# Attention on one core: transposes and their copies ahead of values and exponentials, the gathered unit right behind the maxima

## The chip, the cores and the metric

The kernel runs on one core of one Trainium2 chip. The metric is the device time of one execution in microseconds (us). Engines are named as in the profile: PE is TensorE's matmul, DVE is VectorE, ACT is ScalarE, POOL is GpSimd, SP is SyncE.

## What is computed

Eight images of 512 channels by 32x32 pixels go through four layers, each with a group norm in front and a residual sum behind. The change lies in the second one, an attention with 8 heads of 64 channels over the 1024 pixels:

```
qkv = einsum('oc,bchw->bohw', qkv_w, x);  q, k, v = split(qkv, 3)      # to heads: b p n d, p = 8, n = 1024, d = 64
rp = (h_pos + w_pos) as p n d
scores = einsum('bpnd,pmd->bpnm', q, rp) + einsum('bpnd,bpmd->bpnm', q, k)
attn = softmax(scores, axis=-1)
out = einsum('bpnm,bpmd->bpnd', attn, v)
x = x + out                                                              # back to channels by pixels
```

The third layer (a deformable convolution) gathers 9 neighbourhoods for each of 16 groups from a table in HBM. The kernel spreads that gather of one image over the stages of others, so it runs beside the attention too.

## The kernel before, in words

**Images and stages.** `program` (L1871) runs image 0 and image 1 through three layers, then a loop over images 2 to 7. From image 1 on, a gather of an earlier image runs beside all stages. The gather is cut into 128 units of 9 indirect DMAs (`Gather`, L90). POOL issues them (`plan`, L131). It is paced by grants: in the attention ACT gives one behind each of its first 8 copies and one with each of the 64 exponentials (`tick`, L324), 72 in all for 30 units (34 in image 1), and POOL's calls are spread evenly over them (270 calls, 3.75 for a grant). Five buffers hold units. POOL waits before a unit until the unit five earlier has been summed (L127). DVE works a unit off in `weigh` (L152): one multiply by the weights (L162) and one reduction (L168), whose end signals `summed`. SP stores a finished tile when its 16 units are summed (`keep`, L177). `Spread` (L228) calls `weigh` so that the units of a stage are spread over its steps.

**The attention** (`layer1`, L989). First a group norm and the values' projection, with ACT copying (L1166). Then 32 steps j: 4 pairs of heads by 8 tiles of 128 queries, both heads r of the pair in one step. Head and tile together make an index i = 2j + r. On four engines, each with an order written out by hand:

- `scores(j)` (PE, L1050): four products for both heads into PSUM banks 0 to 3. It waits until both exponentials of step j-1 are done, as they read the same banks.
- `maximum(i)` (DVE, L1203): negated row maximum of one head's 1024 scores.
- `exponential(i)` (ACT, L1144): exponential with that maximum as bias and the row sum, into one of four tiles E. It gives a grant to POOL.
- `turn(i)` (PE, L1065): eight transposes of E into banks 4 and 5. `turn_copy(i)` takes bank 4 out on DVE (L1210) and bank 5 on ACT (L1134) into ET. The next `turn` writes the same banks, so it waits for both copies.
- `values(c)` (PE, L1075): for a chunk c of two steps, 16 products of vT with ET into bank 6, behind `inverses(c)` (L1091), which spread the inverse row sums in the same bank. `chunk_at(j)` puts them into odd steps from j = 3, the chunk ended two steps earlier.
- `inverse_copy(c)` (ACT, L1155) and `output(c)` (DVE, L1224; in the following even step) take the result out and add it to X.
- `quarter(hp, r)` (PE, L1035): in even steps a quarter of the projection of the next pair's queries and keys into bank 7, taken out by `q_copy` (ACT, L1129) or `k_copy` (DVE, L1190). The last pair has none to make.

A matmul in 32 bits stands in the trace as two instructions, so `scores` is x8, `values` x32 and a quarter x8. The order of one step before:

```
PE    turn(2j-2)  scores(j)  [odd: inverses, values]  turn(2j-1)  [even: quarter]
ACT   copy(2j-2)  exponential(2j)  exponential(2j+1)  [odd: inverse_copy]  copy(2j-1)  [q_copy]
DVE   copy(2j-2)  maximum(2j)  maximum(2j+1)  [invert]  copy(2j-1)  [output]  [k_copy]  spread
```

`turn(2j-2)` and `turn(2j-1)` are of the exponentials of the step before.

Of the kernel before, what the change touches and what calls it, by code (L numbers as in the profile page):

```python
# [17 lines left out]
P = 128  # L18
# [4 lines left out]
PT = N // P  # L23
# [253 lines left out]
class Builder:  # L277
# [711 lines left out]
    def layer1(self):  # L989
        nc, io, PS, X = self.nc, self.io, self.PS, self.X  # L990
        with ExitStack() as ctx:
# [10 lines left out]
            rrow = self.sb(ctx, "rrow", [P, 2 * P])  # L1002
            ov = self.sb(ctx, "ov", [P, 2 * P])
            w_loaded = self.sem("qkv_w_loaded")
            names = ("v_done v_out p_done q_out k_out s_done0 s_done1 max_ready e_ready t_done t_out0 t_out1 o_done0 "
                     "o_done1 rden_ready r_done r_out o_out l1_order").split()
            (v_done, v_out, p_done, q_out, k_out, s_done0, s_done1, max_ready, e_ready, t_done, t_out0, t_out1, o_done0,
             o_done1, rden_ready, r_done, r_out, o_out, order_s) = [self.sem(n) for n in names]
            s_done, o_done = (s_done0, s_done1), (o_done0, o_done1)

            def load(sp):
                sp.dma_start(wq[:], io["qkv_w"][:]).then_inc(w_loaded, 16)
# [17 lines left out]
            with Stage(nc) as block:  # L1030
# [3 lines left out]
                def _(pe):  # L1034
# [29 lines left out]

                    def turn(i):  # L1065
                        pe.wait_ge(e_ready, i + 1)
                        if i:
                            pe.wait_ge(t_out0, i)
                            pe.wait_ge(t_out1, i)
                        for m in range(PT):  # L1070
                            mm = nc.tensor.transpose(PS[:, 4 + m // 4, (m % 4) * P:(m % 4 + 1) * P],  # L1071
                                                     E[i % 4][:, m * P:(m + 1) * P], self.ident[:])
                        mm.then_inc(t_done, 1)

                    def values(c):  # L1075

# [37 lines left out]
                    for j in range(steps + 2):  # L1114
                        if 1 <= j <= steps:
                            turn(2 * j - 2)
                        if j < steps:
                            scores(j)
                        if chunk_at(j) is not None:
                            inverses(chunk_at(j))  # L1120
                            values(chunk_at(j))
                        if 1 <= j <= steps:
                            turn(2 * j - 1)
                        if quarter_at(j):
                            quarter(*quarter_at(j))

                @block.scalar
                def _(act):
                    def q_copy(hp, r):  # L1129
                        act.wait_ge(p_done, 4 * hp + r + 1)  # L1130
                        nc.scalar.activation(q[hp % 2][:, r * NH:(r + 1) * NH], PS[:, 7, :], ACT.Copy)\  # L1131
                            .then_inc(q_out, 1)

                    def turn_copy(i):  # L1134

                        c, r = i // 4, i % 2
                        act.wait_ge(t_done, i + 1)
                        if c >= 2:
                            act.wait_ge(o_done[r], c - 1)
                        nc.scalar.activation(ET[c % 2][r][:, PT // 2:, (i % 4 // 2) * P:(i % 4 // 2 + 1) * P],  # L1140
                                             PS[:, 5, :].rearrange("p (m f) -> p m f", f=P), ACT.Copy)\
                            .then_inc(t_out1, 1)

                    def exponential(i):  # L1144

                        act.wait_ge(max_ready, i + 1)
                        if i >= 4:
                            act.wait_ge(t_done, i - 3)
                        r = i % 2
                        nc.scalar.activation(E[i % 4][:].rearrange("p (h f) -> p h f", h=2),  # L1150
                                             PS[:, 2 * r:2 * r + 2, :], ACT.Exp, bias=nmax[:, i:i + 1],
                                             accum_out=den[:, i:i + 1]).then_inc(e_ready, 1)
                        self.tick(act)

                    def inverse_copy(c):  # L1155

                        act.wait_ge(r_done, 2 * (c + 1))
                        for r in range(2):
                            act.wait_ge(o_done[r], c + 1)
                        if c:  # L1160
                            act.wait_ge(o_out, c)
                        nc.scalar.activation(rrow[:], PS[:, 6, 2 * P:4 * P], ACT.Copy).then_inc(r_out, 1)

                    for m in range(PT):
                        act.wait_ge(v_done, m + 1)
                        nc.scalar.activation(vT[:, m, :], PS[:, m, :], ACT.Copy).then_inc(v_out, 1)  # L1166
                        self.tick(act)
                    for r in range(2):
                        q_copy(0, r)
                    act.wait_ge(v_out, PT)  # L1170
                    for j in range(steps + 2):
                        if 1 <= j <= steps:
                            turn_copy(2 * j - 2)
                        if j < steps:
                            exponential(2 * j)
                            exponential(2 * j + 1)
                        if chunk_at(j) is not None:
                            inverse_copy(chunk_at(j))
                        if 1 <= j <= steps:
                            turn_copy(2 * j - 1)  # L1180
                        if quarter_at(j) and quarter_at(j)[1] < 2:
                            q_copy(*quarter_at(j))

                @block.vector
                def _(dve):
# [23 lines left out]

                    def turn_copy(i):  # L1210

                        c, r = i // 4, i % 2
                        dve.wait_ge(t_done, i + 1)
                        if c >= 2:
                            dve.wait_ge(o_done[r], c - 1)
                        nc.vector.tensor_copy(ET[c % 2][r][:, 0:PT // 2, (i % 4 // 2) * P:(i % 4 // 2 + 1) * P],  # L1216
                                              PS[:, 4, :].rearrange("p (m f) -> p m f", f=P)).then_inc(t_out0, 1)

                    def invert(c):
# [18 lines left out]
                    for j in range(steps + 3):  # L1238
                        if 1 <= j <= steps:
                            turn_copy(2 * j - 2)  # L1240
                        if j < steps:
                            maximum(2 * j)
                            maximum(2 * j + 1)
                        if j >= 2 and j % 2 == 0 and j // 2 - 1 < chunks:
                            invert(j // 2 - 1)
                        if 1 <= j <= steps:
                            turn_copy(2 * j - 1)
                        if j and chunk_at(j - 1) is not None:
                            output(chunk_at(j - 1))
                        if quarter_at(j) and quarter_at(j)[1] >= 2:  # L1250
                            k_copy(*quarter_at(j))
                        if j < steps:
                            spread()
                    spread.end()
                    dve.wait_ge(o_out, chunks)

# [729 lines left out]
```

## Time and profile before

| what | value |
|---|---|
| time of the runs, median of 3 | 17378.5 us (17342.42 to 17394.83) |
| span of the profiled execution | 17321.9 us (its own time outside the span isn't given) |
| busy, share of the span | PE 52%, DVE 56%, ACT 29%, POOL 53% |
| mean granted TensorE clock | 0.726 of full speed |

The busy lines of the page and the slices of the span:

```profile
PE 8991.0 (52%) x32544; PEld 4339.4 (25%) x32544; DVE 9764.5 (56%) x9864; ACT 4946.3 (29%) x13537; POOL 9147.2 (53%) x9221
...
PE   6754554445634564445634555445634556344447
...
POOL 0025655656546664656555664556555665555551
PEclk7976777667766777767866777667866777677778
```

No engine is busy for more than 56% of the span. Each of the 40 slices is 433 us long, so an attention (254 to 440 us) is about one of them, and what bounds it is read from the waits and the order of instructions inside it, not from these shares.

### The profile page before, as it was taken

The numbers are of one execution on the slowest core, as the hardware profiler recorded it, in microseconds if no ns is written. First come the engines' busy times: TensorE is split into PE (matmuls) and PEld (weight loads), VectorE is DVE, ScalarE is ACT, GpSimd is POOL, SyncE is SP. The second block draws the span as 40 slices with busy tenths as digits, with TensorE's granted clock in tenths as the row PEclk, the third lists the DMA queues.
The fourth block names the chain that finished last, engine by engine and source line by source line (L and its number), as shares of the span: only waits on it lengthen the run. The fifth ranks groups of instructions, "written<-read, shape, count | busy, mean of one in ns | idle before, by whom it ended". The sixth has DMA issues, their size and how long they took to land. (4 is left out here: it accounts for less than half of the span.)

```text
span 17321.9 us, 109853 instructions
## 1 busy us (share of the span) xinstructions
PE 8991.0 (52%) x32544; PEld 4339.4 (25%) x32544; DVE 9764.5 (56%) x9864; ACT 4946.3 (29%) x13537; POOL 9147.2 (53%) x9221
## 2 busy tenths in 40 slices
PE   6754554445634564445634555445634556344447
PEld 3322222222312232222312222122312223111113
DVE  7646745476546854477445855467554765433333
ACT  2314421243214421143203422144212432111111
POOL 0025655656546664656555664556555665555551
PEclk7976777667766777767866777667866777677778
DMA  1021112211132112211132112211122111322111
GB/s 58 8 59 42 44 47 66 93 42 51 38 88 66 45 49 62 89 43 52 36 75 79 43 49 59 93 41 46 45 74 78 44 50 51 89 81 71 61 60 45
DMA packets 905633, 1002.04 MB, mean 58 GB/s; under 512 B 697681, under 2 KB 707921, under 8 KB 893074
## 3 DMA queue, kind: packets, MB, share of 16 engines
q0 software_dynamic: 294912, 604.57, 12.3%
q1 hardware_dynamic: 610066, 389.88, 7.4%
q8 instruction: 271, 4.44, 0.1%
q14 instruction: 384, 3.15, 0.1%
HBM read 814.38 MB, written 179.39 MB: 57 GB/s over the span
## 5 line engine op out<-in xcount | busy, mean ns | idle before, releaser
L131 POOL DMA_INDIRECT gat<-corner_tables,idx x9216 | 9146.7, 992 | 7868.6 <-DVE dcn L168 3093.5
L795 PE MATMUL PS<-hc,ident 128*128 128x512 f32 (+2 forms) x4096 | 2018.1, 653 | 483.0 <-DVE hc L839 309.8
L168 DVE TENSOR_REDUCE dcn<-gat 128x32 f32<-128x1152 f32 x1024 | 2162.7, 2112 | 127.2 <-ACT gat L148 83.5
L148 ACT ACTIVATE gat<-gat,wts 128x32 f32<-128x32 f32 x8752 | 1979.4, 308 | 525.6 <-issue 523.8
L862 DVE TENSOR_TENSOR_SCAN hs<-dA,PS 128x1024 f32<-128x1024 f32 x672 | 1531.5, 2279 | 37.5 <-issue 4.4
L162 DVE TENSOR_TENSOR gat<-gat,wts 128x1152 f32<-128x1152 f32 (+3 forms) x1024 | 1093.8, 1068 | 567.1 <-DMA gat<-corner_tables,idx 397.3
L795 PEld LDWEIGHTS PS<-hc,ident 128*128 128x128 f32 x4096 | 1036.8, 286 | 1125.1 <-issue 640.8
L1071 PE MATMUL PS<-ident,E 128*128 128x128 f32 x4096 | 676.5, 313 | 909.1 <-ACT ET L1140 484.0
L1216 DVE COPY ET<-PS 128x512 f32<-128x512 f32 x512 | 348.7, 681 | 1204.6 <-remote 693.6
L839 DVE TENSOR_TENSOR hc<-hs,PS 128x1024 f32<-128x1024 f32 x672 | 803.0, 1195 | 169.7 <-remote 85.6
L1740 PE MATMUL PS<-late_M,wp 128*32 128x512 f32 x4480 | 640.2, 723 | 458.3 <-DVE wp L1804 202.5
L1071 PEld LDWEIGHTS PS<-ident,E 128*128 128x128 f32 x4096 | 528.1, 160 | 1207.9 <-issue 1021.0
L1150 ACT ACTIVATE E<-PS,nmax 128x1024 f32<-128x1024 f32 x512 | 570.0, 1113 | 847.7 <-DVE nmax L1207 508.6
L774 PE MATMUL PS<-bc1f,pick 96*128 96x512 bf16 x1024 | 402.3, 493 | 761.1 <-DVE hc L839 619.2
L774 PE MATMUL PS<-bc1b,pick 96*128 96x512 bf16 x1024 | 391.8, 481 | 779.6 <-DVE hc L839 653.8
L1207 DVE TENSOR_REDUCE nmax<-PS 128x1 f32<-128x1024 f32 x512 | 602.8, 1217 | 273.8 <-PE PS L1060 218.8
L1085 PE MATMUL PS<-ET,vT 128*64 128x256 f32 x4096 | 591.2, 405 | 160.7 <-issue 156.9
L1060 PE MATMUL PS<-kk,q 64*128 64x512 f32 x2048 | 656.9, 771 | 12.8 <-DVE kk L1201 12.8
L1793 DVE COPY row<-PS 128x512 f32<-128x512 f32 x160 | 110.6, 691 | 859.2 <-remote 528.3
L1045 PE MATMUL PS<-XN,wqkv 128*128 128x512 f32 x1024 | 491.8, 625 | 134.9 <-ACT q L1131 66.0
L812 ACT ACTIVATE dA<-delta1f,A 128x1024 f32<-128x1024 f32 x256 | 293.7, 1147 | 838.4 <-DVE hs L862 702.6
L1770 ACT ACTIVATE row<-PS 128x512 f32<-128x512 f32 x160 | 95.5, 597 | 1493.7 <-PE PS L1740 705.9
(251 smaller groups left out, 11848.4 us busy)
## 6 DMA issues: line engine op xcount, KB each, us to landing
gat<-corner_tables,idx POOLq DMA_INDIRECT x9216
corner_tables<-xp SPq DMA_DIRECT2D x1024, 64.0 KB, 2.2
D<-in_dist_dram SPq DMA_DIRECT2D x8, 4096.0 KB, 12.7
keep_scratch<-X SPq DMA_DIRECT2D x15, 2048.0 KB, 11.6
weighted<-M SPq DMA_DIRECT2D x56, 512.0 KB
late_M<-weighted SPq DMA_DIRECT2D x7, 4096.0 KB
wqkv<-in_qkv_w_dram SPq DMA_DIRECT2D x8, 3072.0 KB, 10.2
X<-keep_scratch SPq DMA_DIRECT2D x12, 2048.0 KB, 14.9
```

What stands on the lines that cost most here:

```text
L131: nc.gpsimd.indirect_dma_start(bd.gat[n % self.NG][:, k * 4 * CG:(k + 1) * 4 * CG], None, bd.rows, bass.IndirectOffsetOnAxis(ap=bd.idx[:, ...
L148: ins = nc.scalar.activation(block, block, ACT.Copy, scale=weights[:, i:i + 1])
L162: nc.vector.tensor_tensor(v, v, wv, ALU.mult).then_inc(self.prod, 1)
L168: nc.vector.tensor_reduce(bd.dcn[m % 2][:, g * CG:(g + 1) * CG], gat[:].rearrange("p (k c) -> p c k", c=CG), AX.X, ALU.add).then_inc(self. ...
L774: mm = nc.tensor.matmul(PS[:, bank + i, j * p.hl:(j + 1) * p.hl], self.pick[:, row:row + 1].to_broadcast([3 * BC, P]), p.bc[:, pos], start ...
L795: mm = nc.tensor.matmul(PS[:, p.ybank(d, h), 0:p.hl], self.ident[:], src[:, j, h * p.hl:(h + 1) * p.hl], start=(c == 0 and j == 0), stop=( ...
L839: nc.vector.tensor_tensor(hc[u % 2][:], hs[u % 2][:], Cb, ALU.mult).then_inc(hc_ready, 1)
L862: nc.vector.tensor_tensor_scan(h_, a_, b_, 0.0, ALU.mult, ALU.add).then_inc(scanned, 1)
L1060: mm = nc.tensor.matmul(PS[:, 2 * r + m, :], q[hp % 2][rows, nt * P:(nt + 1) * P], kk[hp % 2][rows, m * NH:(m + 1) * NH], start=True, stop ...
L1071: mm = nc.tensor.transpose(PS[:, 4 + m // 4, (m % 4) * P:(m % 4 + 1) * P], E[i % 4][:, m * P:(m + 1) * P], self.ident[:])
L1207: nc.vector.tensor_reduce(nmax[:, i:i + 1], PS[:, 2 * r:2 * r + 2, :], AX.XY, ALU.max, negate=True).then_inc(max_ready, 1)
L1740: mm = nc.tensor.matmul(PS[32 * j:32 * j + 32, h, :], wp[:, 4 * s + j, :], M[:, 4 * s + j, h * NH:(h + 1) * NH], start=(s == 0), stop=(s = ...
```

## The change

PE's transposes of both indices of a step now stand ahead of inverses and values, and a set of eight is made of two halves, each with its own signal and with a wait for the one copy of its bank. ACT's and DVE's second copies stand ahead of the exponentials and the maxima. DVE's call of `spread` stands behind `output` and ahead of `k_copy`. Which engine takes out which bank, the sizes, the buffers and the numbers of instructions stay, apart from waits.

```diff
@@ -1002,11 +1002,13 @@
             rrow = self.sb(ctx, "rrow", [P, 2 * P])
             ov = self.sb(ctx, "ov", [P, 2 * P])
             w_loaded = self.sem("qkv_w_loaded")
-            names = ("v_done v_out p_done q_out k_out s_done0 s_done1 max_ready e_ready t_done t_out0 t_out1 o_done0 "
+            names = ("v_done v_out p_done q_out k_out s_done0 s_done1 max_ready e_ready t_done0 t_done1 t_out0 t_out1 o_done0 "
                      "o_done1 rden_ready r_done r_out o_out l1_order").split()
-            (v_done, v_out, p_done, q_out, k_out, s_done0, s_done1, max_ready, e_ready, t_done, t_out0, t_out1, o_done0,
+            (v_done, v_out, p_done, q_out, k_out, s_done0, s_done1, max_ready, e_ready, t_done0, t_done1, t_out0,
+             t_out1, o_done0,
              o_done1, rden_ready, r_done, r_out, o_out, order_s) = [self.sem(n) for n in names]
             s_done, o_done = (s_done0, s_done1), (o_done0, o_done1)
+            t_done, t_out = (t_done0, t_done1), (t_out0, t_out1)
 
             def load(sp):
                 sp.dma_start(wq[:], io["qkv_w"][:]).then_inc(w_loaded, 16)
@@ -1064,13 +1066,13 @@
 
                     def turn(i):
                         pe.wait_ge(e_ready, i + 1)
-                        if i:
-                            pe.wait_ge(t_out0, i)
-                            pe.wait_ge(t_out1, i)
-                        for m in range(PT):
-                            mm = nc.tensor.transpose(PS[:, 4 + m // 4, (m % 4) * P:(m % 4 + 1) * P],
-                                                     E[i % 4][:, m * P:(m + 1) * P], self.ident[:])
-                        mm.then_inc(t_done, 1)
+                        for a in range(2):
+                            if i:
+                                pe.wait_ge(t_out[a], i)
+                            for m in range(PT // 2 * a, PT // 2 * (a + 1)):
+                                mm = nc.tensor.transpose(PS[:, 4 + a, (m % 4) * P:(m % 4 + 1) * P],
+                                                         E[i % 4][:, m * P:(m + 1) * P], self.ident[:])
+                            mm.then_inc(t_done[a], 1)
 
                     def values(c):
 
@@ -1116,11 +1118,11 @@
                             turn(2 * j - 2)
                         if j < steps:
                             scores(j)
+                        if 1 <= j <= steps:
+                            turn(2 * j - 1)
                         if chunk_at(j) is not None:
                             inverses(chunk_at(j))
                             values(chunk_at(j))
-                        if 1 <= j <= steps:
-                            turn(2 * j - 1)
                         if quarter_at(j):
                             quarter(*quarter_at(j))
 
@@ -1133,11 +1135,11 @@
 
                     def turn_copy(i):
 
-                        c, r = i // 4, i % 2
-                        act.wait_ge(t_done, i + 1)
+                        c, r, at = i // 4, i % 2, i % 4 // 2 * P
                         if c >= 2:
                             act.wait_ge(o_done[r], c - 1)
-                        nc.scalar.activation(ET[c % 2][r][:, PT // 2:, (i % 4 // 2) * P:(i % 4 // 2 + 1) * P],
+                        act.wait_ge(t_done1, i + 1)
+                        nc.scalar.activation(ET[c % 2][r][:, PT // 2:, at:at + P],
                                              PS[:, 5, :].rearrange("p (m f) -> p m f", f=P), ACT.Copy)\
                             .then_inc(t_out1, 1)
 
@@ -1145,7 +1147,7 @@
 
                         act.wait_ge(max_ready, i + 1)
                         if i >= 4:
-                            act.wait_ge(t_done, i - 3)
+                            act.wait_ge(t_done1, i - 3)
                         r = i % 2
                         nc.scalar.activation(E[i % 4][:].rearrange("p (h f) -> p h f", h=2),
                                              PS[:, 2 * r:2 * r + 2, :], ACT.Exp, bias=nmax[:, i:i + 1],
@@ -1171,13 +1173,12 @@
                     for j in range(steps + 2):
                         if 1 <= j <= steps:
                             turn_copy(2 * j - 2)
+                            turn_copy(2 * j - 1)
                         if j < steps:
                             exponential(2 * j)
                             exponential(2 * j + 1)
                         if chunk_at(j) is not None:
                             inverse_copy(chunk_at(j))
-                        if 1 <= j <= steps:
-                            turn_copy(2 * j - 1)
                         if quarter_at(j) and quarter_at(j)[1] < 2:
                             q_copy(*quarter_at(j))
 
@@ -1209,11 +1210,11 @@
 
                     def turn_copy(i):
 
-                        c, r = i // 4, i % 2
-                        dve.wait_ge(t_done, i + 1)
+                        c, r, at = i // 4, i % 2, i % 4 // 2 * P
+                        dve.wait_ge(t_done0, i + 1)
                         if c >= 2:
                             dve.wait_ge(o_done[r], c - 1)
-                        nc.vector.tensor_copy(ET[c % 2][r][:, 0:PT // 2, (i % 4 // 2) * P:(i % 4 // 2 + 1) * P],
+                        nc.vector.tensor_copy(ET[c % 2][r][:, 0:PT // 2, at:at + P],
                                               PS[:, 4, :].rearrange("p (m f) -> p m f", f=P)).then_inc(t_out0, 1)
 
                     def invert(c):
@@ -1238,19 +1239,18 @@
                     for j in range(steps + 3):
                         if 1 <= j <= steps:
                             turn_copy(2 * j - 2)
+                            turn_copy(2 * j - 1)
                         if j < steps:
                             maximum(2 * j)
                             maximum(2 * j + 1)
                         if j >= 2 and j % 2 == 0 and j // 2 - 1 < chunks:
                             invert(j // 2 - 1)
-                        if 1 <= j <= steps:
-                            turn_copy(2 * j - 1)
                         if j and chunk_at(j - 1) is not None:
                             output(chunk_at(j - 1))
+                        if j < steps:
+                            spread()
                         if quarter_at(j) and quarter_at(j)[1] >= 2:
                             k_copy(*quarter_at(j))
-                        if j < steps:
-                            spread()
                     spread.end()
                     dve.wait_ge(o_out, chunks)
```

## Rows read from the trace of the kernel before

**Rows 1.** The page's first line.

```profile
span 17321.9 us, 109853 instructions
```

**Rows 2.** Windows, first to last exponential of an attention: images 0, 5, sum of eight.

```profile
core 0: us, PE busy (x) PEld busy (x) DVE busy (x) ACT busy (x) POOL busy (x), PEclk, DMA share, GB/s
710.10:964.30 254.20, 226.18 (x1425) 131.87 (x1425) 132.97 (x178) 117.96 (x210) 0.00 (x0) 0.97 0.00 1
...
10258.10:10667.00 408.90, 275.10 (x1423) 153.47 (x1423) 215.44 (x228) 116.64 (x209) 224.74 (x227) 0.80 0.13 38
...
sum 3121.10, PE 2146.78 PEld 1200.81 DVE 1650.57 ACT 936.13 POOL 1598.90; mean PE 268.35 PEld 150.10 DVE 206.32 ACT 117.02 POOL 199.86
```

**Rows 3.** Waits of DVE and ACT, whole span: us in total, times, longest.

```profile
DVE ET L1216 <- remote: 693.6, 81, 14.2
...
DVE nmax L1207 <- remote: 35.5, 22, 4.2
...
ACT rrow L1162 <- remote: 734.1, 80, 17.6
```

**Rows 4.** Timeline of image 0, an odd and an even step: start, us, engine, line.

```profile
742.13 1.04 PE L1071 MATMUL PS<-ident,E 128*128 128x128 f32 x8
...
743.10 1.99 PE L1060 MATMUL PS<-kk,q 64*128 64x512 f32 x8
...
745.02 0.66 PE L1099 MATMUL PS<-ident,rden 128*64 128x128 f32 x8
745.12 2.35 DVE L1207 TENSOR_REDUCE nmax<-PS 128x1 f32<-128x1024 f32 x2 [0.77 <-PE PS L1060]
745.50 3.62 PE L1085 MATMUL PS<-ET,vT 128*64 128x256 f32 x32
746.38 1.11 ACT L1150 ACTIVATE E<-PS,nmax 128x1024 f32<-128x1024 f32 x1 [2.57 <-DVE nmax L1207]
...
749.06 1.09 PE L1071 MATMUL PS<-ident,E 128*128 128x128 f32 x8
...
750.19 0.69 DVE L1216 COPY ET<-PS 128x512 f32<-128x512 f32 x1 [2.71 <-PE PS L1071]
...
754.82 3.60 PE L1045 MATMUL PS<-XN,wqkv 128*128 128x512 f32 x8
755.25 1.11 ACT L1150 ACTIVATE E<-PS,nmax 128x1024 f32<-128x1024 f32 x1 [2.57 <-DVE nmax L1207]
...
758.26 0.82 PE L1071 MATMUL PS<-ident,E 128*128 128x128 f32 x6
```

**Rows 5.** Timeline of image 5, from an even step's exponential to the next one's.

```profile
10413.62 1.11 ACT L1150 ACTIVATE E<-PS,nmax 128x1024 f32<-128x1024 f32 x1 [3.36 <-DVE nmax L1207]
...
10417.65 1.41 POOL L131 DMA_INDIRECT gat<-corner_tables,idx  x1 [0.30 <-issue]
...
10418.17 1.35 DVE L162 TENSOR_TENSOR gat<-gat,wts 128x1152 f32<-128x1152 f32 x1
10419.36 0.97 POOL L131 DMA_INDIRECT gat<-corner_tables,idx  x1 [0.30 <-issue]
...
10421.59 0.68 DVE L1216 COPY ET<-PS 128x512 f32<-128x512 f32 x1
...
10423.44 1.11 ACT L1150 ACTIVATE E<-PS,nmax 128x1024 f32<-128x1024 f32 x1 [5.14 <-DVE nmax L1207]
10423.55 1.09 PE L1071 MATMUL PS<-ident,E 128*128 128x128 f32 x8
...
10431.88 0.94 POOL L131 DMA_INDIRECT gat<-corner_tables,idx  x1 [0.30 <-issue]
10435.58 0.69 DVE L1216 COPY ET<-PS 128x512 f32<-128x512 f32 x1 [11.04 <-remote]
...
10436.64 1.94 PE L1071 MATMUL PS<-ident,E 128*128 128x128 f32 x8 [11.99 <-ACT ET L1140]
10438.51 3.65 PE L1060 MATMUL PS<-kk,q 64*128 64x512 f32 x8
...
10443.45 1.11 ACT L1150 ACTIVATE E<-PS,nmax 128x1024 f32<-128x1024 f32 x1 [4.24 <-DVE nmax L1207]
```

## Prediction, made before the result

> **What bounds the kernel now.** I read the page's span first [rows 1], then the windows from the first to the last exponential of each image's attention [rows 2]. The reader is to see that image 0, which has no gather beside it, needs 254.2 us for 32 steps, and image 5, taken as the type of the other seven, 408.9 us. All eight make 3121.1 us, so the seven take 2866.9 us, 18% of the span with image 0: that is all the change can touch. PE's busy time differs little (226 and 275 us), so the 155 us between them are mostly waits.
>
> The waits say which [rows 3]. VectorE's copy of transposes (L1216) waited 693.6 us in 81 places for a signal that came long after the instruction that sends it ("remote"), and ScalarE's inverse copy (L1162) 734.1 us in 80. The maxima (L1207) waited in this way only 35.5 us. Both long waits are for PE work behind or in the values. I call such a place a hold, and count 80 of them in 7 images of 16 chunks (a chunk is two steps, an odd one with values and an even one): 80 chunks with a hold, 32 without, and 16 in image 0.
>
> The timelines give the anatomy. In image 0 [rows 4], one chunk runs from the first transposes of an odd step at 742.13 to those two steps later at 758.26: 16.13 us. PE is in it nearly all the time, but the odd step's second transposes stand behind values (749.06), and their two copies (750.19) stand between them and the next step. In image 5 [rows 5] the same transposes are issued at 10423.55, their copy starts at 10435.58. In between POOL issues gather calls, the last at 10431.88; the signals came 3.70 us after that. I read a hold as ending with POOL's run, and a run as ending when the calls granted by the two exponentials of each step are used up. So one held chunk is POOL's run plus the way from the release to the next even step's exponential, 10435.58 to 10443.45: 7.87 us. After the hold PE is also at the lower clock level (1.2 GHz): eight transposes take 1.94 us for 1.04 to 1.09, scores 3.65 for 1.99.
>
> **The change, part by part.** Nothing is added or removed but waits: the same matmuls, copies and gather units in another order. No DMA is moved on a queue; the unit's end signal, which lets POOL reuse a buffer and SP store a finished tile, comes earlier. Durations are of the profiled execution, whose span is 17321.9 us; the page gives no time outside it, and I take the 56.6 us by which the median of the runs (17378.5) lies above as unchanged.
>
> *Without a gather.* From the start S of the scores in an odd step: PE goes on 1.92 later (743.10 to 745.02), now with transposes 0.97 (742.13 to 743.10), inverses 0.48, values 3.56 (745.50 to 749.06), and the next first transposes 0.97, whose copies nothing waits for: the next scores start at S+7.90. In an even step the projection takes 3.44 (754.82 to 758.26): 1.92+0.97+3.44+0.97 = 7.30. The other way is longer than now but not last: half a set of transposes gives its copy 1.13-4x0.12 = 0.64 after the start (749.06 to 750.19 is 1.13 for eight), so VectorE copies at S+2.56, its maxima start at S+3.25 instead of S+2.02 (0.69 for the copy), the exponential 1.26 behind (745.12 to 746.38), and two of 1.11 end at S+6.7 [rows 4]. Sum 15.20 for 16.13: 0.93 x 16 chunks = **15 us** less. Here a wait of 2.7 us (copies behind values) goes, and PE itself is late next.
>
> *A chunk without a hold, with a unit in each step.* Odd to even: now 8.87 (746.38 to 755.25), plus 1.00, since the unit (10418.17 to 10421.59, 3.42) starts behind the copy at 750.88, ends at 754.30 and puts another copy in front of the maxima due at 753.99, 1.26 ahead of 755.25 [rows 4, 5]: 9.87. Changed: maxima end 1.09 behind the exponential's start, unit to 4.51, copy to 5.20, PE free for the second transposes at 7.90-4.51+1.92 = 5.31, then 0.64+0.69+1.26: 7.90. Gain 1.97. Even to odd the unit costs more: between it and the next maxima stand two copies and half a set of transposes (0.69+0.64+0.69), where one copy stood, and one copy left the place ahead of it: 2.02-0.68-0.68 = 0.66 lost on today's 9.82 (10413.62 to 10423.44). Net 1.3 x 32 = **42 us** less. The projection's copy for keys, now behind the unit, was behind or ahead of it on the same engine and still ends before the copies; ScalarE's second copy, now queued ahead of the exponentials, waits for transposes that end before the maxima do, so the exponentials do not see it.
>
> *A held chunk.* The trace shows no step in this order under a hold, so I bound it. At the release the copies of the odd step are done, for its transposes now stand ahead of values. What remains depends on how far PE got. If it issued one more set of transposes behind values, as it does now at 10423.55, then scores 3.65, half a set 0.64, copy 0.69, maxima 1.26 remain: 6.24 for 7.87, gain 1.63. If the scores got through as well: two copies 1.38, half a set at the lower clock 0.97, maxima 1.26: 3.6, gain 4.2. If the transposes did not get through, 1.87 more than the first: 8.11, loss 0.24. I take the first, which is what that row shows: 1.63 x 80 = **130 us** less, ends +340 and -19.
>
> *Given back in held chunks.* A unit that today often stands behind a release, with POOL at rest, will stand inside POOL's run. Beside the multiply (10418.17) one call took 1.41 and the next came 1.71 later, against 0.94+0.30 [rows 5]: 0.47 per unit, at one unit a chunk **37 us** more; ends 0 and the whole multiply, 1.35 x 80 = 108. The Trainium skill (SBUF — State Buffer, "Who interferes with whom") says that a tensor_tensor has no two-port mode and takes only the read interface, while writing descriptors needs the write one, so the gather should not feel it: by that rule this term would be 0 and the forecast 37 us lower; the row disagrees, and I keep the row. And the 0.66 of the even step puts the odd exponentials at 10.5 behind the even ones, after POOL has used the first grant; this matters where the step also has a key copy, half of them: 0.66 x 40 = **26 us** more (ends 0 and 53).
>
> Sum: 15+42+130-37-26 = 124 us less, 17378.5-124 = 17254.5, forecast **17255**. A difference under 0.3% (52 us) is about what a measurement of this kernel can't tell from none.
>
> **The rivals.** *Holds swallow the gain.* They stop PE before the transposes behind values, the way from release to exponential is 8.11, and the two losses stay: 15+42-19-37-26 = -25, so 17404. For it: a hold begins somewhere in the values, and PE issues nothing behind 10423.55 for 12 us. Against: that set itself was issued at full speed. Chance 0.20.
>
> *Slower: the copy ahead of the maxima is caught.* The maxima now stand behind a copy that needs PE's signal from the half set behind the scores. If a hold begins that early, some forty matmuls sooner than today, the odd exponentials wait for the end of the even step's grant: calls for 7.5 x 1.25 = 9.4 us, release 12.2 behind the even exponential, odd exponentials at 14.1 (0.69+1.26); their own grant then holds values until 26.3, and 6.24 on: 32.5 for 29.83. That is 2.7 x 80 = 216 slower, less 57 gained elsewhere, plus 37: 17575. Against: signals of the scores, eight matmuls earlier, are hardly ever late (35.5 us, against 693.6) [rows 3]. Chance 0.11.
>
> *Holds become rarer,* since odd exponentials come later, POOL's run breaks and PE's signals flow in the break: half of them gone is 40 x 8.6 (693.6/81) = 344, with the rest some 470 us: 16910. Nothing in the rows shows that a break of under 1 us is enough. Chance 0.07.
>
> **How the numbers follow.** The forecast has 0.62. It reaches up to 15+42+340 = 397 less (16981); the first rival and the spread of the runs (17342.4 to 17394.8, 26 each way) carry the upper end to 17440. Left out are the slower rival and the rare holds, 0.18. Faster by over 0.3%: 0.58 of the forecast (the small rest falls within) and 0.07, 0.65. Within: 0.04 and 0.14 of the first rival, 0.18. Slower: the rest of that, 0.06, and 0.11, 0.17.
>
> **What would show it.** Image 0's window near 239 us, with the maxima's start 3.2 behind the scores and no wait of L1216 or L1140 for transposes behind values. In the others the remote wait of L1216 in odd steps should now fall on the next step's first copy, the unit (L162) should stand beside POOL's run during a hold, and from the release to the next exponential there should be 6.2 us. I am wrong if the maxima show long remote waits (slower rival), if first transposes start only after the release (first rival), if there are clearly fewer than 80 holds, or if POOL's run does not end where the hold ends.

## The result, and the profile after

The changed kernel took 17246.6 us (median of 5 runs, 17184.8 to 17253.2) against 17378.5 us before: ratio 0.9926, 95% interval [0.9907, 0.9945]. The forecast was 17255 us. That the total agrees doesn't show that its terms do, so they are checked one by one below.

First the page of the changed kernel, its span and its busy line:

```profile
span 17245.0 us, 109853 instructions
...
PE 9108.0 (53%) x32544; PEld 4392.2 (25%) x32544; DVE 9764.0 (57%) x9864; ACT 4950.1 (29%) x13537; POOL 9165.7 (53%) x9221
```

The instructions are the same in number, and so is the work of VectorE and ScalarE. The span is 77 us shorter than in the profile of before [rows 1], the median 132 us: the profiled execution of before was one of its quicker ones. Only 1.6 us of the changed kernel's profiled run (17246.6 us) lie outside its span, so the 56.6 us that the forecast put there were mostly scatter between executions.

The windows from first to last exponential of images 0 and 5, and the sum of all eight, which answer to [rows 2]:

```profile
711.30:955.40 244.10, 230.17 (x1435) 134.72 (x1433) 132.33 (x179) 119.80 (x210) 0.00 (x0) 0.96 0.00 1
...
10205.00:10613.70 408.70, 299.86 (x1435) 162.82 (x1433) 217.04 (x230) 118.19 (x210) 227.07 (x231) 0.80 0.13 38
...
sum 3091.20, PE 2288.71 PEld 1255.61 DVE 1663.05 ACT 948.76 POOL 1638.41; mean PE 286.09 PEld 156.95 DVE 207.88 ACT 118.60 POOL 204.80
```

Image 0 fell by 10.1 us, the sum by 29.9 us. What follows the last exponential up to the last output (from its start, in the timelines) fell by another 39 us over the eight images (238.3 to 199.3 us). In a second pair of profiles, below, it fell by 16 us (230.9 to 214.9).

Then the waits of the changed kernel, to be held against [rows 3]:

```profile
DVE ET L1217 <- remote: 978.5, 125, 19.7
...
DVE nmax L1208 <- PE PS L1062: 17.1, 8, 2.1
...
ACT rrow L1164 <- remote: 845.6, 87, 22.0
```

The maxima hardly wait any more, as their own engine now comes late instead (the second copy stands in front of them). The copies wait longer for late signals than before, and in more places: 125 instead of 81, and the inverse copies in 87 instead of 80. The holds did not get rarer; they got more.

The timeline of image 0, an odd step and the beginning of two even ones' scores, against [rows 4]:

```profile
745.88 1.99 PE L1062 MATMUL PS<-kk,q 64*128 64x512 f32 x8
...
747.80 1.09 PE L1073 MATMUL PS<-ident,E 128*128 128x128 f32 x8
748.49 0.69 DVE L1217 COPY ET<-PS 128x512 f32<-128x512 f32 x1 [1.36 <-PE PS L1073]
...
749.10 2.35 DVE L1208 TENSOR_REDUCE nmax<-PS 128x1 f32<-128x1024 f32 x2
749.31 3.62 PE L1087 MATMUL PS<-ET,vT 128*64 128x256 f32 x32
...
752.86 1.09 PE L1073 MATMUL PS<-ident,E 128*128 128x128 f32 x8
...
753.88 1.99 PE L1062 MATMUL PS<-kk,q 64*128 64x512 f32 x8
...
761.13 1.13 PE L1062 MATMUL PS<-kk,q 64*128 64x512 f32 x4
```

From the odd step's scores the next ones follow after 8.00 us (forecast 7.90), and the next after 7.25 (7.30); the maxima start 3.22 behind the scores (3.25). PE runs through without a gap.

The timeline of a held chunk, here in image 6, against [rows 5]:

```profile
12304.27 1.11 ACT L1152 ACTIVATE E<-PS,nmax 128x1024 f32<-128x1024 f32 x1 [0.35 <-DVE nmax L1208]
...
12310.48 1.06 PE L1073 MATMUL PS<-ident,E 128*128 128x128 f32 x8 [0.75 <-DVE ET L1217]
...
12311.96 3.74 PE L1087 MATMUL PS<-ET,vT 128*64 128x256 f32 x30
...
12314.02 1.35 DVE L162 TENSOR_TENSOR gat<-gat,wts 128x1152 f32<-128x1152 f32 x1
...
12314.91 1.27 POOL L131 DMA_INDIRECT gat<-corner_tables,idx  x1 [0.30 <-issue]
...
12316.49 0.94 POOL L131 DMA_INDIRECT gat<-corner_tables,idx  x1 [0.30 <-issue]
...
12317.14 0.81 PE L1073 MATMUL PS<-ident,E 128*128 128x128 f32 x3
...
12321.57 4.05 PE L1062 MATMUL PS<-kk,q 64*128 64x512 f32 x5
12322.73 0.94 POOL L131 DMA_INDIRECT gat<-corner_tables,idx  x1 [0.30 <-issue]
12326.01 2.08 PE L1062 MATMUL PS<-kk,q 64*128 64x512 f32 x3 [0.39 <-issue]
12326.27 0.69 DVE L1217 COPY ET<-PS 128x512 f32<-128x512 f32 x1 [8.77 <-remote]
...
12329.78 2.35 DVE L1208 TENSOR_REDUCE nmax<-PS 128x1 f32<-128x1024 f32 x2
...
12331.03 1.11 ACT L1152 ACTIVATE E<-PS,nmax 128x1024 f32<-128x1024 f32 x1 [0.35 <-DVE nmax L1208]
```

The second transposes (12310.48) are out of the way before values. The unit runs during the hold, beside POOL's run. Behind values PE does not stand still: it lets the next eight transposes (three of them shown) and five of the eight matmuls of the next scores through, a few at a time. The release at 12326.27 comes 3.54 us after the last call of the run, and the next exponential 4.76 us after the release, where it took 7.87 in the chunk of [rows 5].

### The profile page after: what moved, and what is told of

Read it like the earlier page. It is cut to its first block and busy times, and to the rows that moved or that the text cites. A ratio compares the mean times of both kernels' runs of the same rounds, so it can differ in the third digit from the quotient of the medians.

```text
span 17245.0 us, 109853 instructions
## 1 busy us (share of the span) xinstructions
PE 9108.0 (53%) x32544; PEld 4392.2 (25%) x32544; DVE 9764.0 (57%) x9864; ACT 4950.1 (29%) x13537; POOL 9165.7 (53%) x9221
## 5 line engine op out<-in xcount | busy, mean ns | idle before, releaser
L862 DVE TENSOR_TENSOR_SCAN hs<-dA,PS 128x1024 f32<-128x1024 f32 x672 | 1531.8, 2279 | 36.0 <-DVE PS L830 4.6
L1073 PE MATMUL PS<-ident,E 128*128 128x128 f32 x4096 | 713.6, 315 | 726.3 <-DVE ET L1217 297.3
L1062 PE MATMUL PS<-kk,q 64*128 64x512 f32 x2048 | 708.3, 761 | 48.1 <-issue 33.3
L1142 ACT ACTIVATE ET<-PS 128x512 f32<-128x512 f32 x512 | 305.5, 597 | 1222.0 <-PE PS L1073 576.4
L1047 PE MATMUL PS<-XN,wqkv 128*128 128x512 f32 x1024 | 535.6, 672 | 132.7 <-issue 70.2
```

What stands on the lines that cost most here:

```text
L862: nc.vector.tensor_tensor_scan(h_, a_, b_, 0.0, ALU.mult, ALU.add).then_inc(scanned, 1)
L1062: mm = nc.tensor.matmul(PS[:, 2 * r + m, :], q[hp % 2][rows, nt * P:(nt + 1) * P], kk[hp % 2][rows, m * NH:(m + 1) * NH], start=True, stop ...
L1073: mm = nc.tensor.transpose(PS[:, 4 + a, (m % 4) * P:(m % 4 + 1) * P], E[i % 4][:, m * P:(m + 1) * P], self.ident[:])
```

## Experiments

Two theories stood at the start. Theory 1 is the forecast's: the gain is the shorter way from the end of a hold to the next exponential, and holds end with GpSimd's run of calls. Theory 2, the rival: the gain comes from VectorE's unit, whose earlier end frees a gather buffer sooner; over the whole span GpSimd's wait for the unit's reduction fell from 3093 to 2827 us.

Ratios are to the kernel before, run in the same session; sessions differ (it took 17162 us in the first of these, 17354 and 17362 in the others, and 17378 with the result), so total times are compared as ratios. Where holds are counted, a hold is an odd step whose inverse copy starts over 3 us after the exponential in front of it ended, in the timeline of images 1 to 7. Only chunks with another step behind them are counted, 14 in each image, 98 in all: behind the last two of an image no exponential follows in that attention. (The 84 holds and the 6.3 us of the expectations take in most of these as well.) "The way" is from the inverse copy's start to the next exponential, the median over the holds. The even-to-odd steps are 98 too, the first ones of each image's 15.

### Both kernels a second time

> The kernel before, unchanged, as a second profiled sample. Both theories: no difference in time (17340 to 17395 us), eight attentions from first to last exponential of 3080 to 3150 us in sum, inverse copies held in 60 to 75 places, and about 7.9 us from a release to the next exponential. If its attentions scatter by more than 60 us against the first profile, the sums of single profiles cannot carry an argument of that size.

> The changed kernel, unchanged, as the control for the others. 17185 to 17255 us; eight attentions of 3050 to 3110 us in sum from first to last exponential; 80 to 90 held inverse copies with a median of 6.3 us from the release to the next exponential, in two groups near 3.6 us (the next scores went through during the hold) and 6.5 us (they did not).

The kernel before: ratio 0.9998 [0.998, 1.0016], 61 holds (55 in the first profile), way 7.96 us (7.96). The changed kernel: 0.9926 [0.9901, 0.9951], the same as the first time, 77 holds (74), way 4.69 us (6.22). The sums of the windows, before and then changed:

```profile
sum 3118.60, PE 2136.54 PEld 1195.95 DVE 1650.16 ACT 938.10 POOL 1601.19; mean PE 267.07 PEld 149.49 DVE 206.27 ACT 117.26 POOL 200.15
```

```profile
sum 3013.10, PE 2248.81 PEld 1240.29 DVE 1664.99 ACT 950.70 POOL 1633.18; mean PE 281.10 PEld 155.04 DVE 208.12 ACT 118.84 POOL 204.15
```

This pair differs by 105.5 us, the first by 29.9: the changed kernel's own two profiles are 78 us apart, more than expected. So no sum of one profile is used below to weigh a part under 80 us. The two groups of ways are there: in the first profile of the changed kernel 21 of 74 lie between 3 and 4 us and 25 between 6 and 7; in the second 34 of 77 and 12. They stand at the forecast's two cases, 3.6 and 6.24 us.

Not all holds end some 3 to 4 us behind a run. The medians from the start of the last call to the release are 3.75 and 3.79 us in the kernel before and 3.62 and 3.32 in the changed one, but 13 of 55 and 15 of 61 holds, then 14 of 74 and 20 of 77, end less than 2 us after the start of a call, many of them in the middle of a run. No run here shows what ends these.

### The unit alone

```diff
# the kernel before, VectorE's loop
+                        if j < steps:
+                            spread()
                         if 1 <= j <= steps:
                             turn_copy(2 * j - 1)
...
-                        if j < steps:
-                            spread()
```

> The kernel before with only VectorE's gathered unit moved, right behind the maxima and ahead of the second copy; PE, ScalarE and the transposes as before. Theory 1 (the gain is the shorter way from a hold's release to the next exponential, because the odd step's copies are done before the hold): that way stays at 7.9 us, image 0 stays at 253 us, time within 0.3% of before, 17330 to 17430 us. Theory 2 (the gain is the earlier unit, which frees a gather buffer sooner, as GpSimd's wait for the unit's reduction fell from 3093 to 2827 us): most of the gain shows, 17240 to 17300 us, and that wait falls by 200 us or more.

Ratio 1.0023 [1.0005, 1.0041]: slightly slower. GpSimd's wait is down all the same, and the windows are longer:

```profile
POOL gat L131 <- DVE dcn L168: 2652.5, 373, 50.4
```

```profile
sum 3208.10, PE 2126.07 PEld 1210.05 DVE 1667.93 ACT 941.24 POOL 1683.18; mean PE 265.76 PEld 151.26 DVE 208.49 ACT 117.66 POOL 210.40
```

The wait fell by 244 us against the same kernel in that session (2896.1) and the time did not fall with it. So a shorter wait for the unit does not by itself bring time, and theory 2 has no support here. It is not quite out: the way did not stay at 7.9 us as theory 1 had it, but rose to 9.52, so about 1.6 us in each of 80 holds may hide a gain. That the unit now stands ahead of the copy for which the next transposes wait is the likely reason, and was not tried by itself.

The run shows something else: the unit alone brings more holds, 80 for 55 and 61. GpSimd's wait for a buffer beside image 5's attention is, in the two profiles of the kernel before, in this run and in the changed kernel:

```profile
POOL gat L131 <- DVE dcn L168: 61.4, 9, 16.7
...
POOL gat L131 <- DVE dcn L168: 57.7, 8, 16.8
...
POOL gat L131 <- DVE dcn L168: 15.9, 6, 7.4
...
POOL gat L131 <- DVE dcn L168: 29.0, 5, 14.6
```

Over images 1 to 7 it is 418 and 393 us before, 112 here, and 147 and 151 in the two profiles of the changed kernel: with buffers free sooner, GpSimd's runs have fewer breaks. And here 49 of the 80 holds end less than 2 us after the start of a call, so that most of them do not end behind a run.

### The set of eight in one piece, and the unit behind the key copy

```diff
# the changed kernel, PE (the copies' waits follow)
-                        for a in range(2):
-                            if i:
-                                pe.wait_ge(t_out[a], i)
-                            for m in range(PT // 2 * a, PT // 2 * (a + 1)):
+                        if i:
+                            pe.wait_ge(t_out0, i)
+                            pe.wait_ge(t_out1, i)
+                        for m in range(PT):
...
```

> The changed kernel with the set of eight transposes in one piece again: one signal after all eight, both copies awaited before the next set. Theory 1: VectorE's second copy and with it the maxima come 0.5 us later at full clock and 1.0 us at the lower one, so the way from a release to the next exponential grows from 6.3 to about 7 us, and 84 holds with some unheld steps give 40 to 90 us: 17270 to 17330 us; image 0 stays within 3 us, as PE is last there. Theory 2 (the unit's place makes the gain): no difference to the changed kernel, 17185 to 17255 us.

Ratio 0.9939 [0.9917, 0.996]. The way's short group moved from 3 to 4 us (21 of 74 holds) to 4 to 5 us (21 of 54), as if the half set saved about a microsecond there; image 0 took 245.6 us for 244.1. In time it is 0.13% (22 us) behind the changed kernel, less than expected and within both intervals: what the split is worth stays open. The holds lie elsewhere, too: 54 in odd steps, but 36 even-to-odd steps over 13 us, where the changed kernel had 19 and 12.

```diff
# the changed kernel, VectorE's loop
-                        if j < steps:
-                            spread()
                         if quarter_at(j) and quarter_at(j)[1] >= 2:
                             k_copy(*quarter_at(j))
+                        if j < steps:
+                            spread()
```

> The changed kernel with VectorE's unit behind the copy of keys again, as before, in the steps that have one. Theory 1: the unit is off the path of a hold, and in unheld even steps it ends before or after the key copy with the same sum, so no difference to the changed kernel: ratio 0.990 to 0.995 to before. If the unit's place carries the gain, it is lost in a fourth of the steps: ratio 0.994 to 0.998.

Ratio 0.9951 [0.9932, 0.997], on the border of the two expectations, and the interval overlaps the changed kernel's: not told apart either.

### Finer grants

```diff
# the changed kernel, ScalarE
-                self.background(block, self.share["attention"], ticks=PT + 2 * steps)
+                self.background(block, self.share["attention"], ticks=PT + 4 * steps)
...
                             .then_inc(t_out1, 1)
+                        self.tick(act)
```

> The changed kernel with a grant for GpSimd also behind each of ScalarE's transpose copies: 136 grants instead of 72 for the same 270 calls, so that the two odd exponentials release 4 calls instead of 7.5. Theory 1 (a hold ends when GpSimd's run ends): about 4.4 us less run behind the odd exponentials in some 84 holds, 200 to 370 us less in the attentions and a time of 16880 to 17050 us. If holds last as long as they do for a reason of PE's own, whatever GpSimd does: no difference, 17185 to 17255 us, and releases no longer follow the last call by 3.6 us.

16933.3 us, ratio 0.9753 [0.9732, 0.9773]: 0.9753/0.9926 = 0.983 of the changed kernel, some 300 us, as theory 1 expected.

```profile
sum 2881.90, PE 2230.69 PEld 1242.72 DVE 1662.06 ACT 946.34 POOL 1741.66; mean PE 278.84 PEld 155.34 DVE 207.76 ACT 118.29 POOL 217.71
```

The windows are 131 and 209 us shorter than in the two profiles of the changed kernel. From the first value copy to the first exponential it is 401.1 us for 524.5 and 516.5, about 120 us less: there each grant released 3.75 calls, now 2. So only part of the some 300 us comes from holds. Their number is about the same (73 for 74 and 77), and the median one still ends 3.33 us after a call, but the run behind the odd exponentials is shorter: an odd-to-even step with a hold takes 15.9 us in the mean for 18.7 and 18.1. No instruction of PE, VectorE or the gather was changed, only when GpSimd may issue. So how long a hold lasts depends on the run.

The same on the kernel before:

> The kernel before with the finer grants of the previous experiment alone (136 for the same 270 calls, the new ones behind ScalarE's transpose copies). Theory 1: holds end with GpSimd's run in this order too, so the part from the first value copy to the first exponential falls by 110 to 125 us in sum as it did there, and the loops by some 100 to 200 us: ratio 0.980 to 0.987 to before. The changed order still wins on top, since the way from a release to the next exponential stays near 7.9 us here (4.6 us there): slower than the changed kernel with fine grants (ratio 0.975) by 60 to 150 us. If the finer grants make the order immaterial, 0.973 to 0.977.

Ratio 0.9841 [0.9819, 0.9862], with a way of 7.52 us against 3.98: much as theory 1 expected. The finer grants are worth 1.6% in the old order, and the new order is worth 0.9% on top (0.9753/0.9841 = 0.991; the intervals are apart).

### All grants of a chunk at the even step's copies

```diff
# the finer grants, ScalarE
-                        self.tick(act)
+                        if i % 4 >= 2:
+                            for _ in range(4):
+                                self.tick(act)
...
                                              accum_out=den[:, i:i + 1]).then_inc(e_ready, 1)
-                        self.tick(act)
```

> The changed kernel with as many grants (136), but those of a chunk all at the two copies of its even step, four each, and none with the exponentials, so that one run of 15 calls starts right behind the release. Theory 1: a chunk is then the run (18.75 us and 0.5 for each unit beside it), 0.7 ahead of it and 3.6 behind it, 23 to 24 us, against 26.3 in held chunks of the fine grants: 50 to 130 us less than those, ratio 0.968 to 0.973. If what counts is how many PE instructions fall into one run, the run now meets scores, transposes and projection of the even step too, PE is caught ahead of the odd exponentials, and the maxima wait for transposes held: slower than the fine grants, ratio above 0.98.

Ratio 0.9828 [0.9809, 0.9846]: slower than the finer grants, the second expectation. Of the 98 even-to-odd steps 46 took over 13 us, where it was 10 with the finer grants; in 35 of the 46 VectorE's longest wait was its copy's for a late ("remote") signal. The windows, and VectorE's copies, which now wait for PE without such a delay in 236 places where the changed kernel had 197:

```profile
sum 2987.40, PE 2256.78 PEld 1243.87 DVE 1664.78 ACT 946.58 POOL 1659.90; mean PE 282.10 PEld 155.48 DVE 208.10 ACT 118.32 POOL 207.49
```

```profile
DVE ET L1219 <- PE PS L1073: 655.8, 236, 10.4
```

This is the forecast's slower rival come true in another kernel: PE is caught ahead of the odd exponentials. In the changed kernel the run starts later, with the even exponentials.

### Fewer units beside the attention

```diff
# the changed kernel, units beside images 2 to 7
-        "steps": 8, "scan": 45, ... "attention": 30
+        "steps": 8, "scan": 51, ... "attention": 24
```

> The changed kernel with 24 instead of 30 gather units beside the attention of images 2 to 7 and 6 more beside the scan. Theory 1: 54 calls of 1.25 us fewer per attention, and as the holds follow GpSimd's run, the attentions of images 2 to 7 get 45 to 67 us shorter each, 270 to 400 us in sum. If holds do not follow the run, an attention only loses the six units' work on VectorE, 20 us at the most, 120 us in sum. The scan pays between 6 units of VectorE work (3.2 us each, 115 us in sum) and the whole gain, so the total may go either way; the attentions decide.

The window of image 5 and the sum:

```profile
10313.90:10635.80 321.90, 250.72 (x1435) 142.80 (x1433) 200.18 (x220) 118.61 (x210) 183.33 (x186) 0.90 0.14 39
...
sum 2619.70, PE 2056.61 PEld 1165.67 DVE 1559.18 ACT 950.45 POOL 1356.77; mean PE 257.08 PEld 145.71 DVE 194.90 ACT 118.81 POOL 169.60
```

Images 2 to 7 sum to 1947.2 us, for 2407.0 and 2336.6 in the changed kernel: 389 to 460 us less, where the run is 54 x 1.25 x 6 = 405 us shorter and the units' work on VectorE 120 us at the most. That is theory 1 in size, at or above its upper end of 400. The total is 0.9987 [0.9974, 0.9999], slower than the changed kernel: from its first to its last scan instruction (L862) the scan took 5295 us over the eight images for 4787 and 4752, so it took back more than the attention gave, and more than expected.

### More PE instructions

```diff
# the changed kernel, PE
+                        for again in range(4):
-                        for a in range(2):
-                            for r in range(2):
+                            for a in range(2):
+                                for r in range(2):
```

> The changed kernel with the four small products of the inverses made four times over (the same result each time): 24 matmuls and as many weight loads more per chunk, 1.5 us of PE at most, ahead of values. Theory A (a hold begins when so many PE instructions have fallen into a run): PE is caught earlier in the values, the next scores get through a hold less often, the median from a release to the next exponential rises from 5.0 to 6.3 us to 6.5 us or more, and the time rises by 80 to 250 us over the changed kernel: ratio 0.997 to 1.007 to before. Theory B (a hold begins at a point of the run, whatever PE has done): only chunks without a hold get 1.5 us longer, 20 to 40 us in sum, ratio 0.993 to 0.996, and that median stays.

17643.1 us, ratio 1.0165 [1.0139, 1.0191]: over 2% slower than the changed kernel, more than either theory had. The window of image 0, and the sum:

```profile
711.30:973.70 262.40, 248.52 (x1783) 153.99 (x1783) 132.34 (x179) 119.85 (x210) 0.00 (x0) 0.96 0.00 1
...
sum 3405.00, PE 2584.52 PEld 1459.46 DVE 1662.96 ACT 955.90 POOL 1616.18; mean PE 323.07 PEld 182.43 DVE 207.87 ACT 119.49 POOL 202.02
```

Without a gather the extra products cost 18.3 us in 16 chunks, 1.1 each. The seven images beside a gather pay 296 and 374 us over the two profiles of the changed kernel, 2.6 to 3.3 us in each of 112 chunks. There are 90 holds for 74 and 77, and the release comes 5.82 us after the last call (median), for 3.62 and 3.32. The way is 5.63 us, between the two profiles of the changed kernel (6.22 and 4.69) and under the 6.5 of theory A. So theory B, by which only unheld chunks pay, is out: it had 20 to 40 us in all. Theory A has the direction; its size and its mark were wrong: what grows is the number of holds and the time from the run's end to the release. That PE's signals stand in a line that is worked off slowly beside a run would fit this, but no run shows it.

## Why the prediction was right, and where it was not

**Image 0.** Forecast 15 us less, measured 10.1 in the first pair of profiles (254.2 to 244.1) and 15.3 in the second (259.4 to 244.1). The chunk came out at 15.25 us for the 15.20 worked out, so the chain was right. Not in the working was the beginning. In the first step there are no values to move, and the second copy ahead of the maxima lengthens it (6.8 us for 5.6). The second step took 9.7 us for 7.2, and that goes with TensorE's clock. The granted clock there was 0.64 to 0.69 of full speed, and the transposes and scores took about as long as at the lower level (1.2 GHz) of [rows 5]; in the first profile of the kernel before the clock stayed at 1.00, and they took 1.07 and 1.99 us. PE had idled just before in both cases, for 2.7 and 3.2 us. The second profile of the kernel before had 0.65 there, and its step took 9.9 us. First the changed kernel, then that second profile:

```profile
719.39 1.97 PE L1073 MATMUL PS<-ident,E 128*128 128x128 f32 x8 [2.72 <-ACT E L1152]
...
721.29 3.78 PE L1062 MATMUL PS<-kk,q 64*128 64x512 f32 x8
```

```profile
718.79 1.94 PE L1071 MATMUL PS<-ident,E 128*128 128x128 f32 x8 [3.24 <-ACT ET L1140]
720.66 3.75 PE L1060 MATMUL PS<-kk,q 64*128 64x512 f32 x8
```

So the second pair, at the same clock, is the fair one for image 0.

**The held chunk.** The step "1.63 us for each hold, between -0.24 and 4.2" was right in its middle and its upper case: the way fell from 7.96 us to 6.22 and 4.69. The two groups near 3.6 and 6.4 us are the cases worked out. The forecast took one of them for all, and 21 of 74 and 34 of 77 holds went to the better one. The argument for it, that PE had issued a set of transposes at full speed behind values, understated what PE lets through: also scores, a few matmuls at a time.

**The number of holds** is the step that failed. "80 chunks with a hold, 32 without" was too many to begin with and was kept as it was. Of the 80 waits of [rows 3], 53 were over 3 us and had another exponential behind them in their image; 13 were shorter, and 14 stood in the last two chunks of an image. In the changed kernel 74 of the 87 are of the long kind. By the count used here holds rose from 55 and 61 to 74 and 77. An odd-to-even step without a hold takes 8.9 and 8.6 us in the changed kernel and one with a hold 18.7 and 18.1 (means), so some 17 more (the means of the two counts) are about 17 x 9.6 = 165 us given back, of the size of the main term: the mean way fell by 2.5 and 2.8 us, in 74 and 77 holds 186 and 219 us. What is left is small: all 98 odd-to-even steps take 1599 and 1571 us, for 1594 and 1676 before. Some 30 us came back where even-to-odd steps were held in 3 to 5 fewer places (24 and 15 over 13 us, then 19 and 12; 8 us each). Why more chunks are held is open. The unit alone, moved in the old order, brought 80 holds and the shorter wait for a buffer that the changed kernel also has, so the earlier unit is a likely cause, though that experiment also delayed a copy. More PE instructions in a run brought more holds too (90). The unheld gain of 42 us can't be told apart, as few such chunks are left: without a hold an odd-to-even step fell from 10.1 and 10.2 us to 8.9 and 8.6, and an even-to-odd one rose, as worked out (9.3 and 9.5 us for 9.1 and 8.8).

**Losses.** The multiply beside POOL's run stretched a call to 1.27 and the next to 1.58 us later (12314.91 to 12316.49), 0.34 instead of the 0.47 taken. That is one call. Over the windows of images 1 to 7, calls that start beside a multiply, with the next right behind, follow each other 0.50 us later than the 1.25 us of others in the mean (153 of them; 0.56 us and 101 before). That makes 77 us for 57, so some 20 us of the 37 forecast.

**The rivals.** Holds swallowing the gain: the way says no. The slower rival can't be read from the maxima's late signals, as the forecast proposed, because the copy ahead of them now takes the wait. Read from the steps themselves, even-to-odd steps over 13 us became no more frequent than before (19 and 12 for 24 and 15), so it did not occur here; it did when the grants were moved, at the place that the forecast names. Rarer holds: the opposite happened. (The forecast's upper end adds up to 17404 + 26 = 17430; it has 17440.)

**Not in the forecast by itself** is the part behind the last exponential of an image, 39 and 16 us shorter in the two pairs; the forecast's 16 chunks for each image take it as two chunks like the others.

So the total was met because an underestimated gain in each hold and an overlooked rise in their number partly cancelled; that it agrees to 8 us is luck. The shorter way is read directly from both pairs of profiles, and the finer grants show in both orders that the length of a hold goes by the run. The unit alone did not bring the gain. The new order of transposes and copies was not run without the unit's move, so how the 0.7% is divided among the parts of the change is argued, not shown.

## What to carry to other kernels

Where a wait ends with another engine's burst, order the waiting engine so that everything that does not need the late signals is done before it: here the copies of a step came out of the way after the hold. Then look at who decides how long the burst is: spreading its permissions finer was worth more than the reordering (1.6% for it alone, 0.7% for the order alone, 2.5% for both), at no cost in instructions on the busy engines. And when a change alters how dense an engine's work is, do not carry over the count of its stalls.

## What the runs showed of the hardware that was not expected

PE's signals come late beside a run of indirect DMAs issued by GpSimd: matmuls stand in the trace as issued, and the engines that wait for them stood idle for 8.6 us in the mean (693.6 us in 81 places in the kernel before). In the median hold the wait ends 3.3 to 3.8 us after the start of the last call; about a fifth to a quarter of the holds of the two kernels end within 2 us of a call instead, and 49 of 80 where the unit alone was moved. What in the chip holds the signals isn't shown by any run here. The delay grew with the number of PE instructions in the one run that tried it: 24 more of the trace's small matmuls in each chunk, with their weight loads, cost 1.1 us without a gather and 2.6 to 3.3 us beside one, and the release moved from 3.3 to 3.6 us to 5.8 us after the last call.
